# Attention stage of a four-layer graph network: loads in shares, fewer key tiles transposed by DMA, another order of the steps

## The reference, cut to what matters

```python
adj = jnp.maximum(adjacency_matrix, jnp.eye(n, dtype=adjacency_matrix.dtype))
keys, queries, values = (jnp.einsum('nj,hjk->hnk', node_matrix, W) for W in (Wks, Wqs, Wvs))
atts = jnp.einsum('hqk,hmk->hqm', queries, keys) / key_dim ** 0.5
atts = atts - 1e+16 * (1.0 - adj)[None, :, :]
atts = jax.nn.softmax(atts, axis=-1)
return jnp.einsum('hqm,hmk,hko->qo', atts, values, Wo)
...
x = _layernorm(x + _L0_gnn_ref(x, adj, ...), axis=-1)
```

## Time and profile before

| what | us |
|---|---|
| median of three executions | 2812.24 |
| the profiled execution, its own time | 2815.72 |
| its span, first to last instruction | 2813.9 |
| PE busy over the span | 2536.2 (90%) |
| DVE busy | 1534.5 (55%) |
| ACT busy | 1388.6 (49%) |
| POOL busy | 1163.6 (41%) |

### The profile page before, as it was taken

How to read it: one execution, slowest core, us unless ns; L and a number is a source line. 1 busy time by engine, 2 the same in 40 slices (tenths; PEclk the granted TensorE clock), 3 DMA queues, 4 the chain that set the end, 5 groups by cost and what they waited for, 6 DMA issues and landing times. The chain is left out here.

```text
span 2813.9 us, 67215 instructions
## 1 busy us (share of the span) xinstructions
PE 2536.2 (90%) x24716; PEld 1564.6 (56%) x24716; DVE 1534.5 (55%) x2860; ACT 1388.6 (49%) x1848; POOL 1163.6 (41%) x879
## 2 busy tenths in 40 slices
PE   7998898988889888898996999799999999979998
PEld 6875566656666566565663444376444444434443
DVE  3447677766777677676772222354454555633222
ACT  3337677767777677676772322223333334323221
POOL 0007687767777677776780032200111111110232
PEclk9999899988999999998998999899999999989999
DMA  3118999999999999999994356411656667742554
GB/s 124 63 57 171 179 174 174 166 174 171 160 173 166 180 173 166 166 181 169 174 157 130 117 196 206 167 48 42 161 153 168 174 178 205 187 127 80 199 196 151
DMA packets 870507, 436.18 MB, mean 155 GB/s; under 512 B 791680, under 2 KB 810112, under 8 KB 859008
## 3 DMA queue, kind: packets, MB, share of 16 engines
q1 hardware_dynamic: 870272, 432.93, 69.6%
HBM read 201.15 MB, written 38.44 MB: 85 GB/s over the span
## 5 line engine op out<-in xcount | busy, mean ns | idle before, releaser
L603 POOL TENSOR_TENSOR att_part_low<-att_scores,att_part_high 128x1024 f16<-128x1024 f32 x352 | 665.7, 1894 | 291.1 <-ACT att_part_high L735 265.2
L766 DVE CUSTOM_DVE_ANT_0 att_scores<-att_slots,att_adj 128x1024 f32<-128x1024 f32 x528 | 568.3, 1092 | 185.8 <-PE att_slots L641 167.1
L719 ACT ACTIVATE att_scores<-att_scores,att_nmax 128x1024 f32<-128x1024 f32 x528 | 531.2, 1037 | 65.8 <-DVE att_nmax L776 63.2
L641 PE MATMUL att_slots<-l_kk,att_q 128*128 128x512 f16 x2112 | 499.8, 376 | 46.4 <-issue 29.0
L1300 PE MATMUL a_ps<-l_y,a_adj 128*128 128x512 f16 (+1 forms) x1936 | 431.6, 382 | 9.0 <-DVE a_adj L1314 4.7
L661 PE MATMUL att_ps_pv<-l_vv,att_far_high 128*128 128x65 f16 x4928 | 270.8, 197 | 115.2 <-DMA att_far_low<-att_part_low 114.8
L661 PEld LDWEIGHTS att_ps_pv<-l_vv,att_far_high 128*128 128x128 f16 x4928 | 258.2, 101 | 159.3 <-DMA att_far_low<-att_part_low 128.6
L1300 PEld LDWEIGHTS a_ps<-l_y,a_adj 128*128 128x128 f16 (+1 forms) x1936 | 183.1, 98 | 257.5 <-issue 42.4
L641 PEld LDWEIGHTS att_slots<-l_kk,att_q 128*128 128x128 f16 x2112 | 190.9, 102 | 223.2 <-issue 77.2
L809 DVE TENSOR_TENSOR att_near_low<-att_ps_t,att_near_high 128x512 f16<-128x512 f32 x352 | 225.7, 681 | 133.5 <-ACT att_near_high L746 133.2
L1045 PE MATMUL edge_ps_o<-l_sup,edge_pt_high 128*128 128x512 f16 x968 | 288.1, 379 | 0.0
(11 more groups left out here) (149 smaller groups left out, 3842.6 us busy)
## 6 DMA issues: line engine op xcount, KB each, us to landing
l_adj<-in_adj_cols SPq DMA_DIRECT2D x44, 1408.0 KB, 6.2
att_adj<-in_adj SPq DMA_DIRECT2D x22, 1354.0 KB, 6.8
l_adj_tiles<-in_adj SPq DMA_DIRECT2D x22, 1354.0 KB, 6.0
p_x_in<-x SPq DMA_DIRECT2D x66, 256.0 KB, 2.6
att_q<-q_rows SPq DMA_DIRECT2D x88, 128.0 KB, 6.1
a_xres<-x SPq DMA_DIRECT2D x44, 256.0 KB, 2.7
scores_rows<-edge_raw SPq DMA_DIRECT2D x8, 842.0 KB, 3.5
p_x_in<-in_x SPq DMA_DIRECT2D x22, 256.0 KB, 2.7
```

The costliest lines, as they stand in the source:

```text
L603: nc.gpsimd.tensor_tensor(out=part[1][:, v, lo:lo + width], in0=sc[:, v, lo:lo + width], in1=part[0][:, v, lo:lo + width], op=ALU.subtract ...
L641: mm = nc.tensor.matmul(slots[:, slot, z:z + w], q[:, u, h % 2, a, h // 2, :], kk[:, h, lo + z:lo + z + w], start=a == 0, stop=a == 1)
L719: nc.scalar.activation(sc[:, v, lo:lo + width], sc[:, v, lo:lo + width], ACT.Exp, bias=nmax[:, v:v + 1]).then_inc(exp_done, 1)
L766: nc.vector.tensor_tensor_reduce(out=sc[:, v, lo:lo + width], in0=slots[:, (NC * h + c) % 2, 0:width], in1=adj[:, u, lo:lo + width], scale ...
```

## The change

Only `attention` and its constants change.

- 12 instead of 14 key tiles go by DMA transpose (`TK = 12`); 10 instead of 8 are transposed on PE, in three groups of 4, 4 and 2. The third group has a PSUM bank of its own, which the output projection now shares (`ps_misc`).
- The far part of the probabilities is 1024 columns and 512 columns (`FAR`). The high half of the first 1024 is made by POOL instead of ACT, that of the 512 by ACT instead of POOL. POOL makes both low halves at the end of its step.
- SP issues high, high, low, low instead of high, low, high, low. The loads come after the transposes of the step and are spread over the 8 steps: four adjacency parts of up to 768 columns at h = 0 to 3, two query loads at h = 4 and 5, the store at h = 6, the residual rows at h = 7.
- The bias is made in four parts (h = 2, 3, 5, 5), directly behind each part's load; the diagonal is applied afterwards (h = 6).
- PE makes the far products before the second and third near group, before piece 2 of the scores, and the near products last. The output transposes and the projection move to the head of steps 5 and 6; the residual and statistics of DVE to the head of step 6.
- ACT and DVE interleave the near halves with exponentials and masks, group order 0, 2, 1.

The constants:

```diff
-TURNED = 2
-TK = PIECES[TURNED][0] // P
-TURN_GROUPS = [list(range(TK, TK + GB)), list(range(TK + GB, T))]
+TK = 12
+FAR = [(0, CHUNK), (CHUNK, TK * P - CHUNK)]
+TURN_GROUPS = [list(range(k, min(k + GB, T))) for k in range(TK, T, GB)]
...
+ADJ_PARTS = [(c, min(6 * P, N - c)) for c in range(0, N, 6 * P)]
+BIAS_STEPS = (2, 3, 5, 5)
...
-        ps_misc = s.ps("ps_misc", [P, BANK])
...
+        ps_misc = ps_t[:, NT - 1, :]
```

SyncE, the step and its loads:

```diff
+            def loads(m, u, h):
...
+                    if h < len(ADJ_PARTS):
+                        if h == 0 and not is_tile(m, u, 0):
+                            sp.wait_ge(slot_free, PER_TILE * t)
+                        load_adj(u1, t + 1, h)
+                    elif h < len(ADJ_PARTS) + 2:
+                        load_q(t + 1, u1, h - len(ADJ_PARTS))
+                if h == 6 and not is_tile(m, u, 0):
+                    norm.store(sp, out_rows, *before(m, u))
+                if h == 7 and not is_tile(m, u, T):
...
+                    for a, made in enumerate((part_high, part_low)):
+                        for c, (lo, width) in enumerate(FAR):
...
+                            wait_apart(sp, made[c], i + 1, pad_clear)
+                            sp.dma_start_transpose(far[a][:, v, k, :], part[a][:, v, lo:lo + width]) \
+                                .then_inc(far_ready[c][v], 16)
+                loads(m, u, h)
```

GpSimd:

```diff
+                    wait_apart(pool, exp_done, NC * i + 1, pad_clear)
                     nc.gpsimd.tensor_copy(part[0][:, v, lo:lo + width], sc[:, v, lo:lo + width]) \
-                        .then_inc(part_high[1], 1)
-                    low(i, v, 1)
+                        .then_inc(part_high[0], 1)
+                for n, bias_h in enumerate(BIAS_STEPS):
+                    if h == bias_h and not is_tile(m, u, T - 1) and not is_tile(m, u, T):
+                        bias(*after(m, u), n)
...
-                if h == 7 and not is_tile(m, u, 0):
+                if h == 6 and not is_tile(m, u, 0):
                     norm.finish(nc, pool, *before(m, u))
...
+                if on(1):
+                    low(i, v, 0)
+                    low(i, v, 1)
```

TensorE, behind the output work at the head of h = 5 and 6:

```diff
                     scores(i, u, h, 0)
                     scores(i, u, h, 1)
                 if on(2):
                     j, _t, _u, h2, _same = unit(m, u, h, 2)
                     turn(j, h2 % 2, 0)
+                if on(3):
+                    k, _t, _u, h3, same = unit(m, u, h, 3)
+                    far_products(k, h3 % 2, h3, same, 0)
+                    far_products(k, h3 % 2, h3, same, 1)
+                if on(2):
                     turn(j, h2 % 2, 1)
...
+                    turn(j, h2 % 2, 2)
                 if on(0):
                     scores(i, u, h, 2)
...
+                    near_products(k, h3 % 2, h3)
```

More of the change, by code:

```diff
@@ L542, in _, with load_q @@
         def _(sp):
[L543 to L549, removed]
+            def load_q(t, u, half):
+                sp.dma_start(q[half * KD:half * KD + KD, u, :, :, :, :].rearrange("p e a j r -> p e (a j r)"),
+                             q_rows[bass.ds(t * P, P), :].rearrange("(e p) n -> p e n", e=2)).then_inc(q_loaded[u], 16)
@@ L555, in loads @@
[L555 to L563, removed]
+                    _m1, u1 = after(m, u)
@@ L622, in step @@
                         .then_inc(o_done, 1)
-                if h == 5 and not is_tile(m, u, T - 1) and not is_tile(m, u, T):
-                    bias(*after(m, u))
-                if h == 7 and not is_tile(m, u, 0):
+                if h == 6 and not is_tile(m, u, 0):
                     norm.finish(nc, pool, *before(m, u))
-            bias(0, 0)
+                if on(1):
+                    low(i, v, 0)
+                    low(i, v, 1)
+            for n in range(len(ADJ_PARTS)):
+                bias(0, 0, n)
             all_steps(pool, step)
@@ L679, in step @@
                 i = t * H + h
+                if h in (5, 6) and not is_tile(m, u, 0):
+                    pe.wait_ge(near_low[NT - 1], T * H if is_tile(m, u, T) else i - 2)
+                if h == 5 and not is_tile(m, u, 0):
+                    pe.wait_ge(o_done, t)
+                    for j in range(J):
+                        mm = nc.tensor.transpose(ps_misc[:, j * P:(j + 1) * P], o[:, j * P:(j + 1) * P], ident[:, :])
+                    mm.then_inc(misc_full, 1)
+                if h == 6 and not is_tile(m, u, 0):
+                    pe.wait_ge(misc_free, 2 * t - 1)
+                    product3(nc, ps_misc[:, :], lambda a, j: ot[:, a, j, :], lambda b, j: wo[b][:, j, :]) \
+                        .then_inc(misc_full, 1)
                 if on(0):
                     if h == 0:
-                        pe.wait_ge(q_loaded[u], 64 * (m + 1))
+                        pe.wait_ge(q_loaded[u], 32 * (m + 1))
                     scores(i, u, h, 0)
@@ L825, in step @@
                     norm.statistics(nc, dve, t - 1)
+                if on(0):
+                    if h == 0:
+                        dve.wait_ge(diag_ready, t + 1)
+                    mask(i, u, h, 0)
+                if h == 5 and not is_tile(m, u, 0):
+                    dve.wait_ge(misc_high, t)
+                    nc.vector.scalar_tensor_tensor(
+                        out=ot[:, 1, :, :], in0=ps_misc[:, :].rearrange("p (j r) -> p j r", j=J), scalar=O_S / V_S,
+                        in1=ot[:, 0, :, :], op0=ALU.mult, op1=ALU.subtract).then_inc(misc_free, 1)
+                if on(2):
+                    j, _t, _u, h2, _same = unit(m, u, h, 2)
+                    near_rest(j, h2 % 2, 0)
+                if on(0):
+                    mask(i, u, h, 1)
+                if on(2):
+                    near_rest(j, h2 % 2, 2)
+                if on(0):
+                    mask(i, u, h, 2)
+                if h == 6 and not is_tile(m, u, T - 1) and not is_tile(m, u, T):
+                    diagonal(*after(m, u))
+                if on(0):
+                    largest(i, h % 2)
+                if on(2):
+                    near_rest(j, h2 % 2, 1)
             rest = len(TURN_GROUPS[-1]) * P
```

202 lines of the change are left out of this document (93 added, 109 removed).

## The result

The changed kernel took 2766.52 us in the median of four runs (2760.71 to 2770.40), the kernel before 2811.84. The ratio is 0.9841, with a 95% interval from 0.9819 to 0.9862: 45 us faster, clear of the noise, where the prediction said 107. The time lies inside the stated range of 2655 to 2785 us, near its slow end.

A forecast was written before the change was run, and what follows sets the result against it. Attention was taken as DMA-bound on average, at PE's pace plus a load-burst stall per tile. Limits of 50.3, 50.1 and 49.5 us plus 4.5% gave 52.6 against 57.8 a tile, over 21 tiles 109 us less: 2705 us, range 2655 to 2785.

The forecast's parts named there:

- the stall: Attention, PE behind each tile's burst of loads: 4 to 5 us plus half clock; spreading should save some 7 us a tile.
- The signs named for it: Steady attention: PE clock above 0.95, far low half waits under 1 us, DMA share 0.95 or so.
- SyncE's queue, 49.5 us: SyncE's issuing of transposes and loads as a limit per attention tile: 8 x 5.56 + 5.0 us; lower bound 40.
- The three limits: Per attention tile, PE 50.3, DMA engines 50.1 and SyncE's queue 49.5 us, with 4.5% added for losses.
- 5.0 us for all loads of a tile: SyncE's queue: time for a tile's loads with the gaps between them, 5.0 us.
- the limit of PE, 50.3 us: PE's attention tile: work 45.6, added transposes 2.1, second stall 2.6; together 50.3 us.
- the price of the turn: Second PE stall at the loop's turn: 3.73 + 1.5 us every second tile, 2.6 a tile, unchanged by the change.
- DMA, 50.1 us: DMA engines per attention tile: loads 7.5 us, transposes 42.6 at 12 of 14 key tiles, down from 57.2 in all.
- rival B: Attention: DMA engines give less, or each load share stalls a little; 54.0 to 55.5 us a tile, 2750 us, chance 0.24.
- Its first form: Rival B: transposes as fast as regular DMAs, so two key tiles save only 3.2 us; DMA term 54.0 us.
- Its second form: Rival B: each step's load precedes its transposes; PE's far products wait, with scores of piece 2 queued behind.
- POOL, ACT and DVE: Attention work per tile put at 40.5, 39.6 and 44.3 us, hidden behind the other limits.

The follow-up runs named there:

- run 2: Changed kernel with its four adjacency and two query loads issued together behind the transposes of h = 0: 2844.91 us, ratio 1.0121.
- run 6: Changed kernel with two DMA transposes a unit, 1536 columns each, instead of four (the merged calls): 2695.40 us, ratio 0.9590.
- run 11: Changed kernel with the merged calls of run 6 and the loop's closing branch announced at the top of each turn: 2664.26 us, ratio 0.9481.
- Run 4: Changed kernel with only the loop's closing branch announced to each engine at the top of a turn: 2769.45 us, ratio 0.9849.
- run 5: Changed kernel with the six adjacency and query loads issued by ACT instead of SyncE: 2725.48 us, ratio 0.9700.
- run 12: As run 11, with DVE's small pass reading one input and ACT making the negative maximum: 2654.70 us, ratio 0.9453.
- run 3: Changed kernel with DVE's small pass reading one input and ACT making the negative maximum: 2773.61 us, ratio 0.9872.
- run 10: Kernel before with loads spread, diagonal and bias later, and merged calls of 1792 columns, still 14 key tiles: 2735.37 us, ratio 0.9715.
- run 9: Kernel before with only merged calls, two DMA transposes of 1792 columns a unit instead of four: 2811.56 us, ratio 1.001.

## Why the prediction was wrong

**Right: the stall.** The burst made the half-clock stall, and the spread removed it (run 2, 17 waits of 5.2 us come back). The signs named for it came: the clock at 0.97, waits of PE of 0.9 us on average, a DMA share of 0.94.

**Wrong: SyncE's queue, 49.5 us.** This is the step that failed. The three limits were said to lie on top of each other, with 4.5% lost between them; in fact the queue stood alone at 55, and the others waited for it. The term was too small by 5.6 us, mostly in the loads. "5.0 us for all loads of a tile" counted eight calls with hardly a gap; the tile of the rows above spent 9.1 on them, 5.3 in the calls and 3.8 in the gaps of 0.2 to 0.3 us before and behind each. The transposes: 8 x 5.56 = 44.5 is the chain of one quiet unit, and the tile spent 46.0, since a call takes 1.19 to 1.26 us in four cases of five and up to 2.5 in the others. The earlier trace rows showed maxima of 4377 and the earlier trace rows one call of 2.02 us; I priced a quiet unit, where a queue that never rests is priced by the mean. Why a call is at times twice as long is not shown. In run 6, with the queue relieved, a tile takes 52.2 us and the program 2695, near the 52.6 and 2705 of the forecast, which points to this term too, though PE's limit was low as well.

**In part right: the limit of PE, 50.3 us.** The two transposes more were priced well: a quiet unit of PE takes 5.62 us instead of 5.37, 0.25 against 0.26 forecast. But with queue and turn relieved (run 11) a tile without the turn takes 49.8 us between diagonals, where the forecast's 45.6 + 2.1 made it 47.7. That the mean of 50.2 us a tile there is the 50.3 forecast is luck: the tiles are 2 us longer, and the announcement takes most of the turn's price away.

**Wrong: the price of the turn.** I put 2.6 us a tile for the second stall, as a part of PE's limit. Run 4 shows that it did not add to the limit at all in the changed kernel: the queue used it. It is on the path only once the queue is relieved: by the diagonals of run 6 the tile with the turn takes 55.9 us on average and the other 49.7, which makes 3.1 us a tile. Announced, in run 11, they take 50.9 and 49.8, and the program is 31 us faster.

**DMA, 50.1 us.** The term is 0.94 x 55.3 = 52.0 in the changed kernel. Two key tiles less took 5.2 us off the 57.2, between the 7.1 of the forecast and the 3.2 of rival B. It is not a price by bytes alone, for the merged calls move the same bytes in 48.0 (run 6) and 47.2 us (0.94 x 50.2, run 11). Rival B came out near the measured time (2750), and it is B that stretched the range so far. Its first form, DMA engines that give less, falls with run 5. Its second form named what PE meets, far products that wait a little in many steps because loads stand ahead of the transposes, but not why: the queue's calls and gaps add up to more than PE's pace. (The page's slices at nine tenths are 5 to 21, where the prediction says 4 to 20; nothing hangs on it.)

**POOL, ACT and DVE.** POOL came out at 41.0 us a tile (779.76 x 55.3 / 1051) and ACT at 39.9, against 40.5 and 39.6. DVE was put at 44.3 and measured 48.7 (925.96 x 55.3 / 1051). The near groups were priced nearly right, but DVE's passes with two inputs in SBUF now meet POOL's: 128x3 at 992 ns instead of 310, and the diagonal of 128x128 at 1.5 us instead of 0.3. Eight passes at 903 instead of 450 ns on average and one diagonal make 4.8 us, all of the 4.4. The Trainium skill says so ("SBUF — State Buffer", Who interferes with whom): such an instruction and one of GpSimd that reads SBUF exclude each other for the whole instruction. The pass that ends with POOL's, above, and the single-input pass at 155 ns (run 12) agree. The change moved POOL's low halves to the end of the step, where this pass stands. In the changed kernel it cost nothing, as run 3 shows; with queue and turn relieved it cost 10 us.

## What to carry to other kernels

The queue that issues DMAs is a resource like an engine: add up its calls with their gaps over a period, by the mean, and look at its waits before trusting any other limit; where they are near nothing, it sets the pace. Here they were 4.7 and 2.3 us in 1050 where merging the calls brought 71 and 59 us (runs 6 and 10), and 31.6 in 1100 where it brought nothing (run 9). Calls whose least price hardly depends on their width should be as wide as the buffers allow, with an eye on the mean, which does rise (1.57 us in the median at 1536 columns, 1.24 at 1024). A fix that brings nothing alone (the loop's turn, DVE's pass) may bring its full worth once the limit above it is gone, so it is tried again after each step.

## What was not expected of the hardware

- A DMA transpose costs its queue 1.19 us at 512 columns, 1.23 at 1024 and 1.28 at 1536, at the least; the median at 1536 is 1.57 for the high halves and 1.45 for the low (run 6), and at 1792 it is 1.83 and 2.71 (run 10).
- The same bytes kept the DMA engines busy for 52.0 us a tile in four calls a unit and 48.0 in two (runs 5 and 6).
- A DMA share near 1 is not a ceiling: 0.99 became 1.05 with 11 GB/s more (run 10).
- The branch that closes the loop of two tiles costs PE up to 4 us of "issue"; announced at the top of the turn, 1.5 to 2.0. The Trainium skill ("Runtime: NRT & Kernel Launch", Instruction fetch mechanics) gives the reason, a fetch of the target's code when a branch is taken and its target is not at hand. No trace here shows the fetch itself; the announcement's effect fits it.
